# The prologue of an attention + FFN kernel, put in a new order on all engines

## The chip, the cores and the metric

The kernel runs on one core of one Trainium2 chip, as one program with one launch. Its time is the device time in microseconds. Three runs of the kernel before took 350.19, 349.46 and 346.96 us; the median is 349.46.

## What is computed

One pre-norm transformer block over x of shape (2, 1024, 128) in f32, with 16 heads of 8 channels:

```python
x = x + attn(layernorm(x))     # q, k, v = xn @ W.T + b; softmax(q k^T + rel_emb[bucket(i-j)] * SCALE, causal) v, then Wo
x = x + ffn(layernorm(x))      # in the reference only expert 0 has weight 1: relu(t @ w1 + b1) @ w2 + b2
# ffn: z = t + that; (z - mean) * rsqrt(var + 1e-5) * gamma + beta
```

The relative bias of a head depends on i - j alone and is constant beyond a distance of 128, so only a band near the diagonal needs it.

## The kernel before, in words

**Data.** The 2048 rows lie in 16 tiles of 128; a *half* is four tiles (512 columns). Attention is cut into 8 groups of 4 heads, 4 groups for each batch (`G`, `GPB`); groups 0 to 3 are batch 0. Q and K are held as a sum of three bf16 parts (`QS`, `NPART`), written to DRAM (`qk_scratch`) and loaded again in the layout of the matmuls: `QA` and `KA` with two buffers each, by half (`load_q` six transfers, `load_k` four). ScalarE makes the first part from PSUM (`first_parts`), the others come from subtractions: for batch 0 on VectorE (`split`, the third query part on GpSimd), for batch 1 on GpSimd, from copies that ScalarE leaves in `R[1]`.

**A group.** For each group, TensorE computes *units* (42, `job`, L1079): scores of a block of queries against "far" keys and "near" keys (with bias, from `NBH`), of which VectorE takes row maxima into `FM`. After unit 11 and unit 40 the maxima of a half are split into two bf16 terms and transposed (units "m0" and "m1"), VectorE copies them to `mrow`, and SP moves them into two rows of `QA` (`move_m`, L454). Then the 12 *steps* of a group run: `scores` (L1107) with these rows as a subtraction, `biases` (L1123) with the table `TT`, Exp on ScalarE (`exps`, L722), `values` (L1138). Units of the next group are placed between the steps of the current one (`SLOTS`; for group 0 `SLOTS0`). Three PSUM banks hold units, so TensorE can be three units ahead of VectorE. Group 0 is the exception: units 0 to 16 run before its first step, 17 to 20 beside the first scores, 21 to 41 in its steps 0 to 2, and units of group 1 in the rest.

**The prologue.** On TensorE: keep-busy matmuls of zeros (`keep_busy`), the relative bias (`task_f`), for each half transposes (`task_t`), Q and K (`task_qks`), V (`task_v`), then the eight matmuls that lay out the reversed bias table `rev` (`task_flip`), whose results `copy_nbh` moves to `NBH`, even ones on ScalarE, odd ones on VectorE. Then the 17 first units, with batch 1's T, Q/K and V tasks at fixed places between them (`T_AT`, `QK_AT`, `V_AT`: the number is the unit before which a task stands). On ScalarE: square roots, copies and first parts, the K loads of group 0, the loads of `rev` (1 MB, into `PT`) and of `TL` (960 KB, into `OT`), from which four copies make `TT` (`copy_tt`), and at the end one Exp on a single element, ahead of which the Exp table is loaded. On GpSimd: memsets of `KA` and of the ones in `VG`, normalisation of batch 1 (`second_batch_norm`), the bias of V, batch 1's parts, bias rows for x. On SP: loads of x, the stores of batch 0, the Q loads, the row move, both halves of group 1 (Q and K), the stores of batch 1.

**What sets the order.** Every engine runs its instructions in the order written and waits on counting semaphores; each wait holds up all that is behind it. `s_qst[b][c]` counts the stores of a half (b batch, c half), `s_mid` the second parts, `s_q3` the third parts, `s_q1` the first parts, `s_xn` normalised halves, `s_xt` their transposes in SBUF, `s_vc` copies of V, `s_r` copies in `R[1]`, `s_zero` memsets. SP's and ScalarE's DMAs go out through queues of their own (q1 and q10 in the profile), GpSimd's through q0. `task_flip` for banks 0 and 1 waited for both V copies, since V stood in those banks.

## Time and profile before

| | us |
|---|---|
| median of three runs | 349.46 |
| the profiled execution: its time | 348.02 |
| its span, first to last instruction | 346.2 |
| mean granted TensorE clock | 0.938 |
| busy: TensorE 291.8, VectorE 273.9, ScalarE 189.5, GpSimd 86.9 | |

The row of busy tenths in 40 slices (8.66 us each) shows the prologue in the first six or seven digits:

```profile
PE   7855687878999998898999889889899888999980
DVE  5565275688889888888989888898899968748895
ACT  2332198305656756765674685585566568762330
POOL 2114999700220202022022011202200001425351
PEclk9995599756999999999999999999999999999996
DMA  7445502540110112022020113123211102000022
```

A digit is the busy share of a slice in tenths, PEclk the granted clock in tenths of full speed. From about slice 11 on the pattern of the groups repeats; the last slices are the output projection and the FFN. Times below are in us from the start of the span.

### The profile page before, as it was taken

The page shows a single profiled execution, that of the slowest core. Times are in us where ns is not written, and L with a number is a line of the kernel's source. Part 1 is how long each engine was busy: PE and PEld are TensorE (multiplying, and loading weights), DVE is VectorE, ACT ScalarE, POOL GpSimd, SP SyncE. Part 2 cuts the span into 40 slices and gives each one's busy share as a digit, 9 for nine tenths or more (in the row PEclk, how much of TensorE's full clock was granted, in tenths as well). Part 3 has the DMA queues.
Part 4 walks back from the last instruction along what each step waited for, and adds up shares of the span by engine and source line. Part 5 has one row for each costly group of instructions (what it writes and reads, how often), then busy time and mean ns, then how long its engine had stood idle before and what let it go on. Part 6 is the DMA issues. An engine that isn't in the chain of part 4 may idle for free.

```text
span 346.2 us, 8324 instructions
## 1 busy us (share of the span) xinstructions
PE 291.8 (84%) x3233; PEld 130.6 (38%) x3235; DVE 273.9 (79%) x968; ACT 189.5 (55%) x262; POOL 86.9 (25%) x127
## 2 busy tenths in 40 slices
PE   7855687878999998898999889889899888999980
PEld 4421332222334234334334423433433343358650
DVE  5565275688889888888989888898899968748895
ACT  2332198305656756765674685585566568762330
POOL 2114999700220202022022011202200001425351
PEclk9995599756999999999999999999999999999996
DMA  7445502540110112022020113123211102000022
GB/s 213 125 126 151 127 0 65 156 139 1 56 56 3 36 23 56 2 54 56 3 57 29 41 27 78 55 34 75 66 22 24 23 4 42 8 0 17 0 62 61
DMA packets 16263, 18.80 MB, mean 54 GB/s; under 512 B 4480, under 2 KB 11776, under 8 KB 16096
## 3 DMA queue, kind: packets, MB, share of 16 engines
q1 hardware_dynamic: 13488, 12.56, 15.3%
q10 hardware_dynamic: 816, 2.96, 3.0%
q0 software_dynamic: 1920, 2.76, 2.7%
q8 instruction: 25, 0.41, 0.5%
q14 instruction: 14, 0.11, 0.1%
HBM read 11.81 MB, written 4.23 MB: 46 GB/s over the span
## 4 chain that ended last, share of the span: by engine, by line
PE 51%; DVE 19%; ACT 14%; issue 6%; POOL 4%; DMA 3%; SPq 1%; ACTq 1%; DVEq 0%; POOLq 0%
PE ps L1145 16%; PE ps L1101 13%; ACT PT L729 9%; PE ps L1133 7%; PE ps L1116 7%; DVE FM L865 6%; DVE junk L872 3%; ACT TT L687 2%; POOL XN L566 2%; PE ps L1178 2%; PE ps L1034 2%; DVE st L929 2%; DVE U L982 1%; PE ps L1087 1%; DMA table_s<-in_table 1%
## 5 line engine op out<-in xcount | busy, mean ns | idle before, releaser
L729 ACT ACTIVATE PT<-ps 128x1024 f32<-128x1024 f32 (+1 forms) x192 | 144.7, 813 | 93.6 <-PE ps L1133 82.1
L865 DVE TENSOR_REDUCE FM<-ps 128x1 f32<-128x512 f32 (+2 forms) x192 | 109.2, 617 | 14.5 <-PE ps L1101 14.0
L872 DVE CUSTOM_DVE_ANT_0 junk<-ps,NBH 128x256 bf16<-128x256 f32 (+1 forms) x256 | 90.3, 400 | 24.7 <-PE ps L1101 24.5
L1101 PE MATMUL ps<-KA,QA 56*128 56x256 bf16 (+3 forms) x544 | 96.9, 292 | 10.6 <-DVE FM L865 7.4
L1116 PE MATMUL ps<-QA,KA 58*128 58x512 bf16 (+3 forms) x384 | 78.0, 334 | 17.5 <-ACT PT L729 14.6
L1145 PE MATMUL ps<-PT,VG 128*16 128x512 f32 (+3 forms) x768 | 87.3, 500 | 0.1
L1101 PEld LDWEIGHTS ps<-KA,QA 56*128 56x128 bf16 x544 | 33.0, 96 | 97.2 <-DVE FM L865 40.6
L420 POOL DMA_DIRECT2D KA<-qk_scratch x24 | 12.9, 542 | 156.7 <-PE ps L1133 156.4
L1116 PEld LDWEIGHTS ps<-QA,KA 58*128 58x128 bf16 x384 | 25.0, 94 | 37.1 <-ACT PT L729 30.2
L1133 PE MATMUL ps<-TT,flb 128*32 128x176 f16 (+4 forms) x1152 | 38.7, 244 | 0.0
L1133 PEld LDWEIGHTS ps<-TT,flb 128*32 128x32 bf16 x1152 | 21.5, 96 | 17.4 <-issue 15.8
L1145 PEld LDWEIGHTS ps<-PT,VG 128*16 128x16 f32 x768 | 21.6, 97 | 6.3 <-ACT OT L734 2.3
L872 DVE DVE_READ_ACCUMULATOR2_ANT FM<- 128x1 f32 x256 | 20.9, 81 | 0.0
L623 POOL TENSOR_SCALAR tmp<-mv 128x4 f32<-128x4 f32 x8 | 2.3, 290 | 66.7 <-DVE mv L932 66.7
L1178 PE MATMUL ps<-QS,late_s 128*128 128x512 f32 x32 | 15.8, 611 | 0.8 <-ACT QS L756 0.8
L1059 PE MATMUL ps<-idle 128*128 128x512 bf16 x29 | 10.7, 534 | 2.2 <-DVE idle L784 1.2
L424 POOL DMA_DIRECT2D KA<-qk_scratch x24 | 12.4, 520 | 0.0
L1034 PE MATMUL ps<-xnT,early_s 128*128 128x512 f32 x16 | 11.1, 834 | 1.4 <-ACT xnT L658 1.4
L658 ACT COPY xnT<-ps 128x512 f32<-128x512 f32 x4 | 2.3, 586 | 16.6 <-PE ps L1028 16.6
L918 DVE RECIPROCAL xnT<-xnT 128x256 f32<-128x256 f32 (+1 forms) x4 | 10.2, 2538 | 0.0
L938 DVE TENSOR_TENSOR QS<-ps,X 128x512 f32<-128x512 f32 x4 | 2.7, 684 | 8.5 <-PE ps L1169 8.5
L734 ACT COPY OT<-ps 128x512 f32<-128x512 f32 x16 | 9.5, 591 | 0.0
(98 smaller groups left out, 261.1 us busy)
## 6 DMA issues: line engine op xcount, KB each, us to landing
QA<-qk_scratch SPq DMA_DIRECT2D x64, 48.0 KB
KA<-qk_scratch POOLq DMA_DIRECT2D x24, 96.0 KB, 2.7
qk_scratch<-QS SPq DMA_DIRECT2D x8, 192.0 KB
qk_scratch<-QS SPq DMA_DIRECT2D x12, 128.0 KB
...
PT<-fr_scratch ACTq DMA_DIRECT2D x1, 1024.0 KB, 4.7
...
```

What stands on the lines that cost most here:

```text
L420: eng.dma_start(KA[64 * e:64 * e + 48, p, c, :, :].rearrange("r h n -> r (h n)"), bass.AP(qk_d, at + e * TILE, [[LINE, 2 * HD], [0, NPART] ...
L424: eng.dma_start(KA[64 * e + 48:64 * e + KS, p, c, :, :].rearrange("r h n -> r (h n)"), bass.AP(qk_d, at + e * TILE + 2 * HD * LINE, [[LINE ...
L729: nc.scalar.activation(PT[:, s % 3, 2 * q:2 * q + 2, off:off + w], ST[:, q, :, off:off + w], ACT.Exp).then_inc(s_exp, 1)
L865: nc.vector.tensor_reduce(FM[:, ib, heads[0]:heads[-1] + 1:2, piece], bank[:, 0:w * len(heads)].rearrange("p (h n) -> p h n", n=w), AX.X, ...
L872: last = nc.vector.tensor_tensor_reduce(junk[:, n % NSM, i, 0:w], bank[:, i * w:(i + 1) * w], nb[:, h, 256 - w:256], 1.0, NEG, ALU.add, AL ...
L1034: nc.tensor.matmul(ps[:, BANK["QK"[qk], b, c], :], (wq_s, wk_s)[qk][:, :], xnT[:, b, c * IC:(c + 1) * IC], start=True, stop=True).then_inc ...
L1059: nc.tensor.matmul(ps[:, bank, :], idle[:, 0:128], idle[:, :], start=True, stop=True)
L1101: last = nc.tensor.matmul(SM[:, n % NSM, i * w + j - j0:i * w + j - j0 + nj], QA[r0:r0 + KS, p, ib // 4, q, (ib % 4) * 128:(ib % 4 + 1) * ...
L1116: last = nc.tensor.matmul(ST[:, q, e, off:off + w], KA[64 * e:64 * e + KST, p, jb // 4, q, (jb % 4) * 128:(jb % 4 + 1) * 128], QA[64 * e:6 ...
L1133: last = nc.tensor.matmul(ST[r0:r0 + 32, q, h % 2, off:off + n], flb[:, 32 * e:32 * e + 32], TT[:, hg, h, u0:u0 + n], start=False, stop=Tr ...
L1145: last = nc.tensor.matmul(OV[32 * h:32 * h + 2 * HD, off:off + w], VG[:, jb, g, h, :], PT[:, s % 3, h, off:off + w], start=(jb == 0), stop ...
L1178: last = nc.tensor.matmul(bank, w1_s[:, f * 128:(f + 1) * 128], tT[:, c % 2, :], start=True, stop=True)
```

## The change

It is a new order of the prologue; the groups from 1 on and the tail keep theirs.

- TensorE: five keep-busy matmuls fewer at the start, the six ahead of the units gone. Flips 0 to 3 stand ahead of batch 0's V, flips 4 to 7 behind it (V now in banks 2 and 3). Units wait for `s_mid` 4 and the table copies, and no longer for the third parts. Batch 1 goes half by half: T before units 2 and 8, Q/K before 4 and 10, V before 13 and 15.
- VectorE: the two splits of half 0 come before the normalisation of half 1; statistics of batch 1 and table copies 1 and 3 (two instead of four) before the splits of half 1, which now include the third query part.
- ScalarE: first parts of half 0, then the loads of `rev` and `TL` and the load of the Exp table, then half 1; six table copies; T of batch 1; only the K load of half 1. Three of the four `TT` copies move into group 0, between the third and fourth Exp pairs.
- GpSimd: memsets early; it waits for half 0's stores and issues the K load of group 0's half 0, later those of group 1.
- SP: key parts are stored singly as each is ready, group 1's Q loads come before the row move, `late` ahead of batch 1's stores, and the wait for these stores moves to the load that fetches group 4.

```diff
-T_AT = {2: 0, 4: 1}
-QK_AT = {6: ((0, 0), (0, 1)), 8: ((1, 0), (1, 1))}
-V_AT = {10: 0, 12: 1}
+T_AT = {2: 0, 8: 1}
+QK_AT = {4: 0, 10: 1}
+V_AT = {13: 0, 15: 1}
 RECIP_AFTER = (6, 14, 22, 30)
...
         s_mid = sem("s_mid")
+        s_lo = sem("s_lo")
         s_r = sem("s_r")
...
         LOADED_Q, LOADED_K = 16 * 6, 16 * 4
-        LOADED = LOADED_Q + LOADED_K
         STORED = 16 * (HP + NPART)
...
-                sp.wait_ge(s_q3[b][qk], c + 1)
+                if (b, c, qk) == (0, 0, 0):
+                    sp.wait_ge(s_lo, 1)
+                else:
+                    sp.wait_ge(s_q3[b][qk], c + 1 if b or qk else c)
                 at = (2 * c + qk) * SIDE + b * 2 * GPB * TILE
...
                     for a in range(NPART):
-                        sp.dma_start(bass.AP(qk_d, at + a * HD * LINE, [[TILE, 2 * GPB], [IC, HD * HP], [1, IC]]),
-                                     QS[:, b, qk, a, c * IC:(c + 1) * IC]).then_inc(s_qst[b][c], 16)
-            def load_half(g, p, c):
-                load_q(sp, g, p, c)
-                load_k(sp, g, p, c)
+                        store_keys(b, c, a)
+            def store_keys(b, c, a):
+                at = (2 * c + 1) * SIDE + b * 2 * GPB * TILE + a * HD * LINE
+                sp.dma_start(bass.AP(qk_d, at, [[TILE, 2 * GPB], [IC, HD * HP], [1, IC]]),
+                             QS[:, b, 1, a, c * IC:(c + 1) * IC]).then_inc(s_qst[b][c], 16)
...
                              F16[:, part, :, :]).then_inc(s_fst[1], 16)
+            def key_part(c, a):
+                ready, count = ((s_q1, 2 * c + 2), (s_mid, 2 * c + 2), (s_q3[0][1], c + 1))[a]
+                sp.wait_ge(ready, count)
+                store_keys(0, c, a)
+            key_part(0, 0)
+            key_part(0, 1)
             store(0, 0, 0)
-            store(0, 0, 1)
+            key_part(0, 2)
             sp.wait_ge(s_qst[0][0], STORED)
             load_q(sp, 0, 0, 0)
+            key_part(1, 0)
             store(0, 1, 0)
-            store(0, 1, 1)
+            key_part(1, 1)
+            key_part(1, 2)
             sp.wait_ge(s_qst[0][1], STORED)
             load_q(sp, 0, 0, 1)
+            load_q(sp, 1, 1, 0)
+            load_q(sp, 1, 1, 1)
             move_m(0, 0, 0)
-            sp.wait_ge(s_zero, 3)
-            load_half(1, 1, 0)
-            load_half(1, 1, 1)
+            sp.dma_start(late_s[:, :], late).then_inc(s_late, 16)
             for c in range(2):
...
                     store(1, c, qk)
-            sp.dma_start(late_s[:, :], late).then_inc(s_late, 16)
-            for c in range(2):
-                sp.wait_ge(s_qst[1][c], STORED)
...
+                if g + 2 == GPB:
+                    for c in range(2):
+                        sp.wait_ge(s_qst[1][c], STORED)
                 load_q(sp, g + 2, p, 0)
...
             nc.gpsimd.memset(mhalf[:, :], -0.5).then_inc(s_p2, 1)
-            for c in range(2):
-                pool.wait_ge(s_mid, 2 * c + 1)
-                q = QS[:, 0, 0, :, c * IC:(c + 1) * IC]
-                nc.gpsimd.tensor_tensor(q[:, 2, :], R[0][:, 2 * c, :], q[:, 1, :], ALU.subtract).then_inc(s_q3[0][0], 1)
+            ones(1)
+            pool.wait_ge(s_zero, 2)
+            nc.gpsimd.memset(VG[:, :, :, :, HD:2 * HD].rearrange("p t g h d -> p (t g h) d"), 1.0).then_inc(s_zero, 1)
+            pool.wait_ge(s_mid, 1)
+            q = QS[:, 0, 0, :, 0:IC]
+            nc.gpsimd.tensor_tensor(q[:, 2, :], R[0][:, 0, :], q[:, 1, :], ALU.subtract).then_inc(s_lo, 1)
+            pool.wait_ge(s_zero, 3)
+            pool.wait_ge(s_qst[0][0], STORED)
+            load_k(pool, 0, 0, 0, s_ldk)
             pool.wait_ge(s_p2, 1)
...
             second_batch_norm(3)
-            pool.wait_ge(s_xn, 4)
-            ones(1)
-            pool.wait_ge(s_zero, 2)
-            nc.gpsimd.memset(VG[:, :, :, :, HD:2 * HD].rearrange("p t g h d -> p (t g h) d"), 1.0).then_inc(s_zero, 1)
             pool.wait_ge(s_rows, 16)
             add_bv(0)
+            load_k(pool, 1, 1, 0, s_ldk)
+            pool.wait_ge(s_qst[0][1], STORED)
+            load_k(pool, 1, 1, 1, s_ldk)
             for k in range(4):
...
-            for c in range(2):
-                pool.wait_ge(s_qst[1][c], STORED)
             for g in range(G - 1):
...
                     load_k(pool, g + 1, 1 - p, 1, s_ldk)
+                if g + 2 == GPB:
+                    for c in range(2):
+                        pool.wait_ge(s_qst[1][c], STORED)
                 if g + 2 < G:
...
             deviation(1)
+            act.wait_ge(s_early, 16)
+            first_parts(0, 0)
             act.wait_ge(s_fst[0], 16)
             act.dma_start(rev[:, :], bass.AP(fr_d, 0, [[H, 128], [1, 256 * H]])).then_inc(s_rev, 16)
-            act.wait_ge(s_early, 16)
-            first_parts(0, 0)
-            turned(0, 1)
-            first_parts(0, 1)
-            copy_v(0)
-            act.wait_ge(s_zero, 1)
-            act.wait_ge(s_qst[0][0], STORED)
-            load_k(act, 0, 0, 0)
-            for i in range(0, 8, 2):
-                copy_nbh(i)
-            act.wait_ge(s_qst[0][1], STORED)
-            load_k(act, 0, 0, 1)
             act.wait_ge(s_fst[1], 32)
...
                               bass.AP(f16_d, part * BW * H, [[H, 64], [1, NEARU * H]])).then_inc(s_tl, 16)
+            act.wait_ge(s_warm, 1)
+            nc.scalar.activation(warm[:, :], eps[:, :], ACT.Exp).then_inc(s_warm, 1)
+            turned(0, 1)
+            first_parts(0, 1)
+            for i in NBH_ACT:
+                copy_nbh(i)
+            copy_v(0)
             turned(1, 0)
+            act.wait_ge(s_zero, 1)
+            act.wait_ge(s_qst[0][1], STORED)
+            load_k(act, 0, 0, 1)
+            first_parts(1, 0)
             turned(1, 1)
-            first_parts(1, 0)
             act.wait_ge(s_tl, 32)
...
             copy_v(1)
-            for hg in range(1, GPB):
-                copy_tt(hg)
-            act.wait_ge(s_warm, 1)
-            nc.scalar.activation(warm[:, :], eps[:, :], ACT.Exp).then_inc(s_warm, 1)
...
-            def group(g, last=False):
+            def group(g, last=False, first=False):
                 for s in range(NSTEP):
+                    if first and s == FIRST_STEP[1] - 1:
+                        for hg in range(1, GPB):
+                            copy_tt(hg)
                     if s + 1 < NSTEP:
...
                 for p in range(2):
-                    group(2 * r + p)
+                    group(2 * r + p, first=r + p == 0)
             group(G - 2)
...
                                                    ALU.add, ALU.subtract))
-                mid = nc.vector.tensor_copy(q[:, 1, :], R_).then_inc(s_mid, 1)
-                if qk:
+                nc.vector.tensor_copy(q[:, 1, :], R_).then_inc(s_mid, 1)
+                if k:
                     dve.wait_ge(s_mid, k + 1)
-                    nc.vector.tensor_tensor(q[:, 2, :], R_, q[:, 1, :], ALU.subtract).then_inc(s_q3[0][1], 1)
+                    nc.vector.tensor_tensor(q[:, 2, :], R_, q[:, 1, :], ALU.subtract).then_inc(s_q3[0][qk], 1)
...
             stats0(1)
-            norm(1)
             nc.vector.tensor_copy(idb[:, :], idf[:, :]).then_inc(s_cst, 1)
             nc.vector.tensor_copy(flb[:, :], flp[:, :]).then_inc(s_cst, 1)
-            for c in range(2):
-                for qk in range(2):
-                    split(c, qk)
-            for i in range(1, 8, 2):
-                copy_nbh(i)
+            for qk in range(2):
+                split(0, qk)
+            norm(1)
             for k in range(2, 4):
                 stats0(k)
+            for i in NBH_DVE:
+                copy_nbh(i)
+            for qk in range(2):
+                split(1, qk)
...
-            dve.wait_ge(s_nbh, 4)
-            dve.wait_ge(s_nbd, 4)
+            dve.wait_ge(s_nbh, len(NBH_ACT))
+            dve.wait_ge(s_nbd, len(NBH_DVE))
             for g, k in STREAM:
...
                 if FLIP_BANK[i] < 2:
-                    pe.wait_ge(s_vc, 2)
+                    pe.wait_ge(s_xt, FLIP_BANK[i] + 1)
                 if i >= 4:
...
             task_f()
-            keep_busy(5, 7)
+            keep_busy(5, 2)
             pe.wait_ge(s_early, 16)
...
             task_qks(0, 1)
-            task_v(0, 0)
-            task_v(0, 1)
             pe.wait_ge(s_f, 2)
...
             pe.wait_ge(s_rev, 16)
-            for i in range(8):
+            for i in range(4):
                 task_flip(i)
+            pe.wait_ge(s_mid, 2)
+            task_v(0, 0)
+            task_v(0, 1)
+            for i in range(4, 8):
+                task_flip(i)
+            def operands(p, half, n):
+                by_act = (p, half) == (0, 1)
+                pe.wait_ge(s_ldqk[p][half], LOADED_Q * n + (LOADED_K if by_act else 0))
+                if n > 1 or not by_act:
+                    pe.wait_ge(s_ldk[p][half], LOADED_K * (n - by_act))
             def job(g, p, k):
...
                         if later and k in HALF_UNITS:
-                            pe.wait_ge(s_ldqk[1 - p][HALF_UNITS[k]], LOADED + LOADED_Q * (load - 1))
-                            if load > 1:
-                                pe.wait_ge(s_ldk[1 - p][HALF_UNITS[k]], LOADED_K * (load - 1))
+                            operands(1 - p, HALF_UNITS[k], load)
                         job(g + later, 1 - p if later else p, k)
...
-            pe.wait_ge(s_q3[0][1], 2)
-            pe.wait_ge(s_nbh, 4)
-            pe.wait_ge(s_nbd, 4)
-            keep_busy(4, 6)
+            pe.wait_ge(s_mid, 4)
+            pe.wait_ge(s_nbh, len(NBH_ACT))
+            pe.wait_ge(s_nbd, len(NBH_DVE))
             for k in JOBS[:JOBS.index(OWN0)]:
...
                     task_t(1, T_AT[k])
-                for c, qk in QK_AT.get(k, ()):
-                    task_qk(1, c, qk)
+                if k in QK_AT:
+                    pe.wait_ge(s_vc, 2)
+                    task_qks(1, QK_AT[k])
                 if k in V_AT:
...
                 if k in HALF_UNITS:
-                    pe.wait_ge(s_ldqk[0][HALF_UNITS[k]], LOADED)
+                    operands(0, HALF_UNITS[k], 1)
                 job(0, 0, k)
...
     order += [("V", 0, 0), ("V", 0, 1)]
-    order += [("T", 1, 0), ("T", 1, 1), ("Q", 1, 0), ("K", 1, 0), ("Q", 1, 1), ("K", 1, 1), ("V", 1, 0), ("V", 1, 1)]
+    for half in range(2):
+        order += [("T", 1, half), ("Q", 1, half), ("K", 1, half)]
+    order += [("V", 1, 0), ("V", 1, 1)]
     bank = {("F", 0, 0): 6}
     bank.update({("T", 0, 0): 0, ("T", 0, 1): 1, ("Q", 0, 0): 2, ("K", 0, 0): 3, ("Q", 0, 1): 4,
-                 ("K", 0, 1): 5, ("V", 0, 0): 0, ("V", 0, 1): 1,
-                 ("T", 1, 0): 2, ("T", 1, 1): 3, ("Q", 1, 0): 0, ("K", 1, 0): 1, ("Q", 1, 1): 2,
-                 ("K", 1, 1): 3, ("V", 1, 0): 0, ("V", 1, 1): 1})
+                 ("K", 0, 1): 5, ("V", 0, 0): 2, ("V", 0, 1): 3,
+                 ("T", 1, 0): 0, ("T", 1, 1): 1, ("Q", 1, 0): 2, ("K", 1, 0): 3, ("Q", 1, 1): 0,
+                 ("K", 1, 1): 1, ("V", 1, 0): 2, ("V", 1, 1): 3})
     return {t: n for n, t in enumerate(order)}, bank
...
 FLIP_BANK = [6, 7, 0, 1, 6, 7, 0, 1]
+NBH_ACT, NBH_DVE = (0, 2, 4, 5, 6, 7), (1, 3)
...
```

## Rows read from the trace of the kernel before

**Rows 1.** The stages of group 0 and of group 1, busy us of each engine, granted clock, DMA.

```profile
57.70:80.40 22.70, 16.60 (x140) 5.67 (x136) 17.31 (x62) 5.21 (x9) 9.13 (x19) 0.64 0.44 127
80.40:102.40 22.00, 21.02 (x258) 7.93 (x254) 19.41 (x65) 13.46 (x18) 4.37 (x8) 0.90 0.13 37
102.40:131.60 29.20, 26.68 (x378) 11.03 (x368) 26.52 (x98) 18.93 (x27) 3.76 (x9) 1.00 0.12 31
```

**Rows 2.** The chain of waits in order of time: start us, us, what.

```profile
52.39 3.81 ACT TT L687 x2
...
56.22 1.28 ACT L720
...
57.73 1.03 ACT PT L729
...
78.03 1.75 DMA QA<-mrow
```

**Rows 3.** Groups of ScalarE's instructions by line, 43 to 57.75 us: busy, mean ns.

```profile
L687 ACT COPY TT<-OT 128x960 f16<-128x960 f16 x4 | 7.6, 1966 | 0.0
...
L663 ACT ACTIVATE QS<-ps,early_s 128x512 bf16<-128x512 f32 x4 | 2.8, 692 | 1.8 <-PE ps L1034 1.7
```

**Rows 4.** TensorE in order of time: start us, us, instructions, idle before.

```profile
7.05 3.17 PE L1059 MATMUL ps<-idle 128*128 128x512 bf16 x7
...
11.74 3.78 PE L1034 MATMUL ps<-xnT,early_s 128*128 128x512 f32 x4 [0.68 <-ACT xnT L658]
...
17.05 1.98 PE L1034 MATMUL ps<-xnT,early_s 128*128 128x512 f32 x4 [0.68 <-ACT xnT L658]
...
29.08 2.72 PE L1059 MATMUL ps<-idle 128*128 128x512 bf16 x6 [0.88 <-DVE NBH L834]
...
40.92 3.38 PE L1034 MATMUL ps<-xnT,early_s 128*128 128x512 f32 x4
...
55.51 0.39 PE L1116 MATMUL ps<-QA,KA 58*128 58x512 bf16 x2 [0.56 <-issue]
```

**Rows 5.** VectorE in order of time, 14 to 53 us.

```profile
14.64 0.75 DVE L813 SCALAR_TENSOR_TENSOR PT<-ps,early_s,QS 128x512 f32<-128x512 f32 x1 [1.09 <-ACT QS L663]
...
17.07 0.43 DVE L815 CAST QS<-PT 128x512 bf16<-128x512 f32 x1
...
20.84 0.83 DVE L815 CAST QS<-PT 128x512 bf16<-128x512 f32 x1
...
52.50 0.40 DVE L860 COPY mrow<-ps 8x512 bf16<-8x512 bf16 x1
```

**Rows 6.** GpSimd in order of time.

```profile
34.90 0.22 POOL L561 TENSOR_SCALAR tmp<-mv 128x4 f32<-128x4 f32 x1
...
36.35 3.14 POOL L566 TENSOR_SCALAR XN<-X,mv,rs 128x128 f32<-128x128 f32 x4
```

**Rows 7.** DMA issues of SP and of ScalarE in order of time.

```profile
18.43 1.97 SPq L446 DMA_DIRECT2D qk_scratch<-QS  x3
...
23.37 1.64 SPq L408 DMA_DIRECT2D QA<-qk_scratch  x4
...
31.84 1.24 ACTq L420 DMA_DIRECT2D KA<-qk_scratch  x2
```

**Rows 8.** The DMA share in three stretches of the prologue.

```profile
12.00:15.00 3.00, 3.00 (x4) 1.13 (x5) 1.88 (x8) 0.69 (x1) 0.00 (x0) 1.00 0.95 336
18.00:23.00 5.00, 3.80 (x22) 2.36 (x21) 4.18 (x8) 2.55 (x4) 1.16 (x1) 1.00 0.59 159
32.00:41.00 9.00, 3.24 (x21) 1.78 (x17) 2.40 (x16) 0.89 (x2) 8.75 (x11) 0.50 0.67 162
```

**Rows 9.** Transfers, KB each and median us from issue to landing (page, part 6).

```profile
PT<-fr_scratch ACTq DMA_DIRECT2D x1, 1024.0 KB, 4.7
...
KA<-qk_scratch POOLq DMA_DIRECT2D x24, 96.0 KB, 2.7
```

**Rows 10.** ScalarE in order of time, inside group 0.

```profile
80.47 1.94 ACT L729 ACTIVATE PT<-ps 128x1024 f32<-128x1024 f32 x2 [7.54 <-PE ps L1116]
```

## The prediction

> **What bounds the kernel now.** I read the stages first, then the chain of waits, then each engine in order of time over the first 60 us. The steady head group takes 29.2 us at full TensorE clock, with all engines close to busy; the first group takes 22.7 + 22.0 us, and its first stretch has a granted clock of 0.64 [rows 1]. The change touches nothing of the seven later groups or the tail. So all it can win lies ahead of the first exponential of group 0 (57.73) and inside that group. The chain of waits just ahead of that exponential is ScalarE alone: table copies and the load of the Exp table [rows 2]. But it is not alone there: TensorE issued the first scores only at 55.51 [rows 4], behind the row copy of the maxima (52.50 to 52.90 on VectorE [rows 5]), SP's move of it and its landing; from those scores to the exponential lie 2.2 us more (the far and near maxima of units 17 to 20 and the bias matmuls). So two chains end within half a us of each other, and taking the table work off ScalarE is worth nothing unless scores(0,0) comes earlier too. What fed both was batch 1: GpSimd finished its last normalisation at 39.5 [rows 6], and behind it and a transpose came Q/K matmuls at 40.92 [rows 4].
>
> **The change, part by part.**
>
> *First half of batch 0.* Seven keep-busy matmuls took 3.17 us, two remain: 2.2 us less, and the normalised tiles are there by then. The transposes start at 7.9 instead of 10.1; with ScalarE's copy they take 1.7 (to 11.74 before), so Q and K of half 0 run 9.6 to 13.3 (3.78 us for their four passes, against 1.98 for the next four: half rate, although the record of the granted clock gives 1.00 so early [rows 4]). ScalarE's first parts end at 12.4 and 14.1 (0.69 each [rows 3]), VectorE's key split (0.75 + 0.43 and a difference of 0.7 [rows 5]) at 16.0. The stores now go out by parts: key part 0 at 14.1, part 1 at 15.4, queries 16.0 to 17.2, key part 2 from 17.2; an issue is 0.6 us. Before, the last of the five was issued from 19.8 (18.43 plus two issues) and the loads followed at 23.37 [rows 7]: 3.55 us. Unhindered they land at 20.8.
>
> *What it puts beside them.* The 1 MB load of the reversed table moves from 11.1 to 14.1 on ScalarE's queue, the two TL loads from 34 to 14.5. Before, the first had the DMA engines to itself (share 0.95 over 3 us = 2.9 us of work), the five stores took 0.59 x 5 = 3.0, TL and the half-1 loads 0.67 x 9 = 6.0, of which I estimate 4 for TL [rows 8]. All three now start near 16: best 20.8, worst 16 + 2.9 + 4 + 3.0 = 26. I take 24, nearer the worst, because the ScalarE queue holds its work first: later than the 23.37 of before by half a us, so the early stores themselves win nothing. The Trainium skill (DMA: Bandwidth & Descriptors, Queues, rings and completion order) says each engine goes round its queues packet by packet; no row shows it, and by it stores with small packets would land near the worst value.
>
> *Second half of batch 0.* norm(1) now waits on VectorE behind the key split: 16.0 + 1.3 = 17.3 (before 13.3). ScalarE issues three loads and the Exp table load (1.28 + 0.2 [rows 2]) from 14.1 to 17.2, just under that cover. Transpose to 18.4, copy to 18.9, Q/K at half rate to 22.4, first parts to 23.5: 3.7 later than before. Flips 0 to 3 follow on TensorE (the reversed table, 4.7 us after its issue [rows 9], is due at 18.8; 3.9 us of slack), VectorE copies 1 and 3 to 25.1 and then splits both sides, 1.9 each, to 28.9. The six copies and two V copies on ScalarE (0.6 apart, an estimate from the 0.69 of a first part that overlaps its neighbour) end at 30.2, the copies alone at 29.0. Last store issue from 29.0, landed by the same 3.55 at 32.6 (before 31.84 [rows 7]): 0.8 lost.
>
> *GpSimd.* It waits for the store at 24, issues four loads (2.1 us, as ScalarE's four at 31.84 [rows 7]) and then normalises: 4.6 each (34.90 to 39.49 for the last [rows 6]): 30.7 and 35.3 instead of 34.9 and 39.5, 4.2 earlier. The ones and VG memsets move into its idle time before 16: nothing, as VG and KA are needed later. What queues behind its new waits is this normalisation; the batch-1 splits after it have stores that only group 4 needs.
>
> *TensorE's units.* The six keep-busy matmuls (2.72 us at 29.08 [rows 4]) go, and units start when copies 4 to 7 are done and half 0 is loaded (24 + 2.1 + 2.7 [rows 9] = 28.8): 29.1 instead of 31.7. T(1,0) at 30.7 to 31.8, its copy to 32.4, the four K load issues on ScalarE wait for 32.6 and take 2.1 (as in [rows 7]) to 34.7; this is the new wait, and first_parts(1,0) is queued behind it: four of 0.65 to 37.3. turned(1,1) to 37.9. Then Q/K(1,1): 3.4 at half rate [rows 4], to 41.3; units 10 to 12 (0.9), V twice (1.1 each, an estimate from the 1.98 of four Q/K passes), units 13 to 15 between (1.2), m0 0.3: 45.9. Row copy 46.7 behind unit 15's maxima, then 2.6 to the scores as before (52.90 to 55.51): 49.3, plus 2.2: the first exponential at 51.5. With the clock up from 38 on, Q/K take 2.0 and the V matmuls less: 50.0. ScalarE, without three table copies (3 x 1.97 [rows 3]) and the table load, finishes copy_v(1) near 45.5 and no longer counts. I take 50.9: **6.8 earlier**. SP issues the query loads of half 0, half 1 and group 1 (2.3 us for six [rows 7]) up to 39.6, then is free for the row move at 46.7; before, that move stood ahead of group 1's loads. Its wait for batch 1's stores, now left to group 2, hid under the second row move, under way at 78.0 [rows 2]: nothing.
>
> *Three table copies in group 0.* 5.9 us of ScalarE ahead of exps(0,4). There ScalarE sat idle 7.54 us before 80.47 [rows 10], behind maxima, m1 and the mrow move (a landing of 1.75 us [rows 2]). 1.6 us of cover is left: cost 0, and up to 5.9 if that idle time vanished. TensorE needs table 1 only at the end of the group.
>
> *Small ones.* A VectorE cast beside a GpSimd subtraction took 0.83 instead of 0.43 [rows 5], twice in the new order at most: 0.8 us, inside VectorE's slack (not in the sum). By the Trainium skill (SBUF — State Buffer, Who interferes with whom) a two-port cast and GpSimd lock each other out; that row agrees.
>
> Sum: 6.8 less. The profiled execution took 348.02 us, 1.44 under the median of 349.46 of the three runs. 348.02 - 6.8 = 341.2; against the median 342.7. I give **342**.
>
> **The rivals.**
> 1. *Loads crowd the stores out* (0.14). If half 0 lands at 26 or later and TL still runs beside the K loads, GpSimd ends near 38 and unit 0 starts past 31; each us goes through to T(1,0) and half of it to the exponential. With a store landing at 27 and half 1 at 36 the exponential is at 54 to 55: 3 to 4 gained, 345 to 346.5. For it: 10 us of transfer work from 16 on [rows 8]. Against: TensorE and ScalarE have 1 to 2 us of slack there.
> 2. *More than the sum* (0.14). TensorE is denser from 29 on, and if its clock stays up, then also group 0's first stretch (0.64 now [rows 1]) shortens: exponential at 49 and up to 4 us inside the group: 10 to 12, so 337 to 338. Against: before, the Q/K matmuls at 40.92 still ran at half rate [rows 4].
> 3. *The table copies become the wait* (0.07). If group 0 gets to exps(0,4) faster by 3 us or more, the 5.9 us stick out and give back 1.5 to 4: 343.5 to 346.
> 4. *Slower* (0.07): the reversed table's load. Flips stand behind it on TensorE, and behind them V, both split copies, the second half's stores, ScalarE's K load and all of batch 1. It decides from 22.4 on, one for one: landed at 29.2 (15 us after issue instead of 4.7) the gain is gone, at 33.5 the time is 353. For it: it has to share with stores and TL. Against: even all the work in line ends at 26, which would cost 3.6.
> 5. *No effect* (0.03): the change doesn't do what it says, because scores(0,0) stay tied to 55.5 by GpSimd's store wait (it equals the old start of its normalisation if half 0 landed at 28); 348 to 349.
>
> Forecast as worked out, 339.5 to 344.5: 0.55. **Range** 337 to 347: late landings (rival 1) and rival 3 reach up to 346.5, the clock (rival 2) down to 337. A measurement of this kernel can tell about 1% from no change. Under 346: the forecast, rival 2, 3 and most of rival 1: 0.82. Within 1%: 0.11. Over 353: 0.07.
>
> **What would show it.** The first exponential (L729's successor) at 50 to 52; half-0 loads beginning at 21 to 26; GpSimd's last normalisation by 36 to 38; no idle time of ScalarE left but little before exps(0,4), with 5.9 us of table copies in it; group 1 starting about 7 earlier and every later group at 29.2 as before. It is wrong if scores(0,0) still come after 54 (then the wait ahead of m0 tells which rival), or if group 0 takes more than 46 us.

## The result, and the profile after

The changed kernel takes 344.68 us in the median of 20 runs, against 349.79 of the kernel before in as many runs beside it: a ratio of 0.9875, 95% interval 0.9851 to 0.9900, so 1.0 to 1.5% less. The profiled execution took 342.63 us with a span of 340.8 (before 348.02 and 346.2).

The page of the kernel after, parts 2 and 4: the granted clock in 40 slices (8.5 us each) in tenths, and the shares of the engines in the chain of work that ended last.

```profile
PEclk9967698969999999999999999999999999999997
...
PE 52%; DVE 22%; ACT 11%; issue 6%; DMA 4%; POOL 3%; SPq 1%; DVEq 0%; POOLq 0%
```

In the slices up to the tenth the clock reads 6, 7 and 6 in the third to fifth and 8 and 6 in the seventh and ninth; before it read 5 and 5 in the fourth and fifth and 7, 5 and 6 from the eighth on.

The stages that answer to [rows 1]: from the first exponential to the one of step 4, from there to the first of group 1, and group 1. Columns: stretch, length, busy us (and count) of PE, PEld, DVE, ACT, POOL, granted clock, DMA share, GB/s.

```profile
53.30:74.10 20.80, 14.36 (x142) 5.13 (x138) 17.08 (x62) 10.65 (x12) 12.13 (x22) 0.83 0.24 72
74.10:96.00 21.90, 20.52 (x253) 7.83 (x252) 19.40 (x65) 13.43 (x17) 4.15 (x8) 0.93 0.13 39
96.00:125.20 29.20, 26.68 (x378) 11.03 (x368) 26.51 (x98) 18.92 (x27) 3.69 (x8) 1.00 0.10 29
```

The gain is ahead of group 1 and nowhere else, and it has two parts. The first exponential comes at 53.30 instead of 57.73: 4.4 earlier. And the stretch from it to the exponential of step 4 is 20.8 instead of 22.7, with a granted clock of 0.83 instead of 0.64: 2.0 more. The second stretch and group 1 have their old lengths (21.9, 29.2). 6.4 in all; the last VectorE instruction is 6.4 earlier too (336.3 + 0.5 against 342.7 + 0.5), and so is the landing of the last output (339.1 against 345.5). But the span is only 5.4 shorter, because it doesn't end with that landing. It ends 0.2 us behind GpSimd's last long instruction, a DRAIN, which took 5.09 us before and 6.07 now. In all 14 traces of this case it is 5.09 where GpSimd issued 48 DMAs (the kernel before, e4) and 6.07 where it issued 60 (all others). The change gives GpSimd twelve more (three K loads of four issues each); no run changed their number alone, so the link is likely and not shown.

Up to 0.5 of the 4.4 may not be the change's: the table's load landed sooner in this execution (TensorE's first use of it at 3.83 instead of 4.38). In e3 below, where that use is at 4.25, the first exponential comes 0.4 later than here.

The 2.0 are those of two single executions. The traced one of the kernel after is the fastest of its 20 (342.63), and the traced one of the kernel before lies 1.8 under its median; how much of the 5.1 us between the medians is clock is not shown.

ScalarE of the kernel after, in order of time: start, us, instructions, idle before them and what ended it.

```profile
14.43 1.28 ACT L719 ACT_TABLE_LOAD   x1 [0.90 <-issue]
...
34.37 0.58 ACT L676 COPY xnT<-ps 128x512 f32<-128x512 f32 x1 [5.79 <-PE ps L1046]
34.79 1.29 ACTq L420 DMA_DIRECT2D KA<-qk_scratch  x2
...
53.30 1.94 ACT L743 ACTIVATE PT<-ps 128x1024 f32<-128x1024 f32 x2 [5.98 <-PE ps L1162]
...
67.19 5.55 ACT L705 COPY TT<-OT 128x960 f16<-128x960 f16 x3
74.08 1.94 ACT L743 ACTIVATE PT<-ps 128x1024 f32<-128x1024 f32 x2 [1.34 <-PE ps L1145]
```

Where ScalarE had no idle time ahead of the first exponential [rows 2, 3], it now waits 5.98 us for TensorE. The three table copies lie in what was 7.54 of idle time [rows 10]; 1.34 is left of it.

TensorE of the kernel after, answering to [rows 4]:

```profile
9.33 3.48 PE L1052 MATMUL ps<-xnT,early_s 128*128 128x512 f32 x4 [0.68 <-ACT xnT L676]
...
30.69 0.40 PE L1130 MATMUL ps<-KA,QA 56*128 56x128 bf16 x4 [4.54 <-DMA KA<-qk_scratch]
33.22 1.11 PE L1046 MATMUL ps<-early_s,XN 128*128 128x128 f32 x4 [2.13 <-POOL XN L579]
...
35.10 3.75 PE L1052 MATMUL ps<-xnT,early_s 128*128 128x512 f32 x4 [0.22 <-ACT xnT L676]
...
41.44 1.96 PE L1052 MATMUL ps<-xnT,early_s 128*128 128x512 f32 x4 [0.34 <-ACT xnT L676]
...
47.75 2.77 PE L1077 MATMUL ps<-idle 128*128 128x512 bf16 x12
51.08 0.39 PE L1145 MATMUL ps<-QA,KA 58*128 58x512 bf16 x2 [0.57 <-issue]
```

TensorE waits for the load of half 0 (4.54) and for GpSimd's normalisation (2.13), and both come of the same landing: SP's queue and GpSimd, answering to [rows 7] and [rows 6].

```profile
16.99 0.61 SPq L454 DMA_DIRECT2D qk_scratch<-QS  x1
25.37 1.56 SPq L408 DMA_DIRECT2D QA<-qk_scratch  x4
...
27.65 0.61 SPq L454 DMA_DIRECT2D qk_scratch<-QS  x1
...
29.55 1.80 SPq L454 DMA_DIRECT2D qk_scratch<-QS  x2
34.73 1.52 SPq L408 DMA_DIRECT2D QA<-qk_scratch  x4
```

```profile
25.98 1.49 POOL L420 DMA_DIRECT2D KA<-qk_scratch  x2 [11.31 <-DMA qk_scratch<-QS]
...
30.03 3.14 POOL L579 TENSOR_SCALAR XN<-X,mv,rs 128x128 f32<-128x128 f32 x4
...
34.60 3.12 POOL L579 TENSOR_SCALAR XN<-X,mv,rs 128x128 f32<-128x128 f32 x4
```

The last store of half 0 is issued at 16.99, and only at 25.37 does SP load it back: 8.4 us, the longest piece of the chain of waits.

### The profile page after: what moved, and what is told of

It is laid out like the page before. It is cut to its first block, busy times and chain, and to the rows that moved or that the text cites. A ratio compares the mean times of both kernels' runs of the same rounds, so it can differ in the third digit from the quotient of the medians.

```text
span 340.8 us, 8308 instructions
## 1 busy us (share of the span) xinstructions
PE 286.3 (84%) x3224; PEld 129.0 (38%) x3224; DVE 272.6 (80%) x967; ACT 190.3 (56%) x264; POOL 92.0 (27%) x138
## 4 chain that ended last, share of the span: by engine, by line
PE 52%; DVE 22%; ACT 11%; issue 6%; DMA 4%; POOL 3%; SPq 1%; DVEq 0%; POOLq 0%
PE ps L1174 15%; PE ps L1130 12%; ACT PT L743 9%; DVE FM L883 8%; PE ps L1145 8%; PE ps L1162 7%; DVE junk L890 4%; PE ps L1052 3%; DMA qk_scratch<-QS 2%; PE ps L1207 2%; DVE st L947 2%; DVE U L1000 1%; PE ps L1116 1%; PE ps L1077 1%; DVE xnT L913 1%
## 5 line engine op out<-in xcount | busy, mean ns | idle before, releaser
L1174 PE MATMUL ps<-PT,VG 128*16 128x512 f32 (+3 forms) x768 | 86.1, 493 | 0.1
L1130 PEld LDWEIGHTS ps<-KA,QA 56*128 56x128 bf16 x544 | 33.3, 95 | 99.8 <-DVE FM L883 42.1
L420 POOL DMA_DIRECT2D KA<-qk_scratch x30 | 16.4, 550 | 163.3 <-PE ps L1162 151.9
L1174 PEld LDWEIGHTS ps<-PT,VG 128*16 128x16 f32 x768 | 21.5, 97 | 6.1 <-ACT OT L748 2.3
L424 POOL DMA_DIRECT2D KA<-qk_scratch x30 | 15.5, 528 | 0.0
L1052 PE MATMUL ps<-xnT,early_s 128*128 128x512 f32 x16 | 13.0, 958 | 1.9 <-ACT xnT L676 1.9
L681 ACT ACTIVATE QS<-ps,early_s 128x512 bf16<-128x512 f32 x8 | 5.5, 692 | 8.2 <-PE ps L1052 8.2
L1046 PE MATMUL ps<-early_s,XN 128*128 128x128 f32 x16 | 4.0, 396 | 6.3 <-DVE XN L820 4.2
```

The source lines that it names most:

```text
L420: eng.dma_start(KA[64 * e:64 * e + 48, p, c, :, :].rearrange("r h n -> r (h n)"), bass.AP(qk_d, at + e * TILE, [[LINE, 2 * HD], [0, NPART] ...
L424: eng.dma_start(KA[64 * e + 48:64 * e + KS, p, c, :, :].rearrange("r h n -> r (h n)"), bass.AP(qk_d, at + e * TILE + 2 * HD * LINE, [[LINE ...
L1052: nc.tensor.matmul(ps[:, BANK["QK"[qk], b, c], :], (wq_s, wk_s)[qk][:, :], xnT[:, b, c * IC:(c + 1) * IC], start=True, stop=True).then_inc ...
L1130: last = nc.tensor.matmul(SM[:, n % NSM, i * w + j - j0:i * w + j - j0 + nj], QA[r0:r0 + KS, p, ib // 4, q, (ib % 4) * 128:(ib % 4 + 1) * ...
L1174: last = nc.tensor.matmul(OV[32 * h:32 * h + 2 * HD, off:off + w], VG[:, jb, g, h, :], PT[:, s % 3, h, off:off + w], start=(jb == 0), stop ...
```

## The experiments

Every kernel is the changed one with one edit, except where it says so. All were timed beside the kernel before; a ratio is to it. The last three columns are from one profiled execution of each, in us from its start; "step 4" is the exponential that stands behind the table copies. There are 5 to 12 runs of each kernel, 20 of the kernel after; beside the experiments the kernel before had medians of 349.62 to 349.71. The profiled execution is the first of its runs and not the middle one: it took 345.43 in e5, 341.86 in e8, and the longest time of its six in e9 (347.22) and e10 (342.36). So a column can be off by the clock of that one run, and the medians decide.

```
kernel              median   ratio [95%]              first exp  step 4  group 1
before              349.79                            57.73      80.47   102.39
after               344.68   0.9875 [0.9851, 0.9900]  53.30      74.08   96.00
e12_old_places      350.92   1.0046 [1.0011, 1.0081]  59.81      82.50   104.43
e4_tables_only      349.15   1.0010 [0.9979, 1.0042]  59.61      80.43   103.42
e3_copies_back      344.11   0.9864 [0.9810, 0.9919]  53.69      76.03   98.01
e1_tl_late          344.57   0.9880 [0.9825, 0.9935]  52.51      73.96   95.89
e2_both_loads       342.40   0.9818 [0.9766, 0.9870]  52.22      73.88   95.81
e5_norm_first       343.49   0.9822 [0.9772, 0.9872]  54.21      76.87   98.80
e7_norm1_first      344.37   0.9863 [0.9828, 0.9897]  53.56      75.41   97.34
e8_best             340.33   0.9755 [0.9709, 0.9800]  50.71      73.26   95.19
e10_tl_last         341.70   0.9786 [0.9735, 0.9837]  50.33      72.89   95.80
e11_busy            340.65   0.9777 [0.9724, 0.9830]  50.24      71.69   93.61
e9_no_idle_mm       345.86   0.9907 [0.9875, 0.9940]  54.57      78.43   100.54
e13_busy_only       344.70   0.9891 [0.9855, 0.9927]  54.16      74.91   96.84
```

**What carries the gain: batch 1's places.** The tasks of batch 1 go back behind the units where they stood, both halves' transposes first.

```diff
-T_AT = {2: 0, 8: 1}
-QK_AT = {4: 0, 10: 1}
-V_AT = {13: 0, 15: 1}
+T_AT = {2: 0, 4: 1}
+QK_AT = {6: 0, 8: 1}
+V_AT = {10: 0, 12: 1}
...
-    for half in range(2):
-        order += [("T", 1, half), ("Q", 1, half), ("K", 1, half)]
+    order += [("T", 1, 0), ("T", 1, 1), ("Q", 1, 0), ("K", 1, 0), ("Q", 1, 1), ("K", 1, 1)]
```

> The changed kernel with batch 1's tasks back at the units of the kernel before (T before units 2 and 4, all Q/K before 6 and 8, V before 10 and 12). Theory P (the placing half by half is what gains: Q/K of half 0 run at 35.1 while GpSimd still normalises half 1): TensorE waits at unit 4 for the normalisation that ends at 37.7, Q/K of half 0 start at 39.5, the first exponential comes 2 to 3.5 us later, at 55.5 to 57, half to three quarters of the gain gone. Rival R (the gain comes from the earlier normalisation and the dropped idle matmuls, whatever the places): under 1 us lost.

350.92 in the median: the whole gain is gone, and a little more. The first exponential is 6.5 us later, about twice what was expected. TensorE of this kernel, in order of time:

```profile
33.69 1.11 PE L1046 MATMUL ps<-early_s,XN 128*128 128x128 f32 x4 [2.69 <-POOL XN L579]
...
38.26 1.11 PE L1046 MATMUL ps<-early_s,XN 128*128 128x128 f32 x4 [2.90 <-POOL XN L579]
...
39.63 3.32 PE L1052 MATMUL ps<-xnT,early_s 128*128 128x512 f32 x4
...
44.87 1.96 PE L1052 MATMUL ps<-xnT,early_s 128*128 128x512 f32 x4 [1.59 <-ACT xnT L676]
...
52.65 0.50 PE L1130 MATMUL ps<-KA,QA 56*128 56x384 bf16 x1 [2.19 <-DVE FM L883]
```

The first transpose comes at 33.69, as late as in the kernel after (33.22); but Q/K of half 0 have to wait for the second half's normalisation (idle 2.90) and start at 39.63 instead of 35.10. That is 4.5 of the 6.5. The rest is lost further on: 1.59 ahead of the second half's Q/K, because ScalarE keeps its new order, with first_parts(1,0) ahead of the second half's copy, and 2.19 ahead of the last unit. That unit is done at 53.15 instead of about 47.1. So e12 is not quite the old placing: it has the old places with ScalarE's order for the new ones. The placement half by half is necessary for the gain, and the order ahead of unit 0 (half 0 early, stores by parts, the loads moved) did not show one without it. That the placement would be enough in the old order wasn't tried.

**Is the table work worth nothing?** Two kernels. The first is the kernel before with only the copies moved into group 0 and the load of the Exp table moved up; the second is the kernel after with the three copies back ahead of the first exponential.

```diff
 # e4, on the kernel before
             copy_v(0)
+            act.wait_ge(s_warm, 1)
+            nc.scalar.activation(warm[:, :], eps[:, :], ACT.Exp).then_inc(s_warm, 1)
...
             copy_v(1)
-            for hg in range(1, GPB):
-                copy_tt(hg)
-            act.wait_ge(s_warm, 1)
-            nc.scalar.activation(warm[:, :], eps[:, :], ACT.Exp).then_inc(s_warm, 1)
...
+                    if first and s == FIRST_STEP[1] - 1:
+                        for hg in range(1, GPB):
+                            copy_tt(hg)
...
 # e3, on the kernel after
             copy_v(1)
+            for hg in range(1, GPB):
+                copy_tt(hg)
...
-                    if first and s == FIRST_STEP[1] - 1:
-                        for hg in range(1, GPB):
-                            copy_tt(hg)
```

> The kernel before with nothing but ScalarE's table work moved: three table copies into group 0, Exp table load right behind the V copies of batch 0. Theory A: the scores at 55.5 and their maxima still hold the first exponential at 57.5, so 0 to 0.3 us gained, ratio 1.000 to the kernel before. Rival T: 5 to 7 us gained, ratio 0.983.

> The changed kernel with the three table copies back ahead of the first exponential (5.7 us on ScalarE from 47.3 on); the Exp table load stays early. Theory A (scores, not ScalarE, set the first exponential; ScalarE sat idle 5.98 us before it): first exponential at 53.3 to 53.5, time unchanged within 0.1 %. Rival T (the table copies out of the way are what the change gains): first exponential 5.7 us later, 1.6 % slower than the changed kernel.

Neither moves the time: 1.0010 with an interval on both sides of 1, and 344.11 against 344.68. ScalarE of e3:

```profile
47.59 5.60 ACT L705 COPY TT<-OT 128x960 f16<-128x960 f16 x3
53.69 1.94 ACT L745 ACTIVATE PT<-ps 128x1024 f32<-128x1024 f32 x2 [0.50 <-PE ps L1161]
...
76.03 1.94 ACT L745 ACTIVATE PT<-ps 128x1024 f32<-128x1024 f32 x2 [7.42 <-PE ps L1144]
```

With the copies back there are still 0.50 us in which ScalarE waits for TensorE: the scores set the start, and the copies fit under them. They are a second chain that ends half a us sooner, as [rows 2, 4] had shown it of the kernel before. In e4 ScalarE, rid of all table work, waits 10.59 us for the scores. They come at 57.38 there, 1.9 later than before, and the exponential with them, at 59.61 and not at the expected 57.5: twelve idle matmuls ahead of them ran at half rate, 5.00 us instead of 2.54 for eleven. Step 4 comes at 80.43, as before, since the stretch behind is shorter by the same amount (20.8 at a granted clock of 0.77). TensorE of e4:

```profile
52.45 5.00 PE L1060 MATMUL ps<-idle 128*128 128x512 bf16 x12
57.38 0.39 PE L1117 MATMUL ps<-QA,KA 58*128 58x512 bf16 x2
```

**Do the table loads crowd the stores out?** e1 issues the two TL loads only behind ScalarE's first two flip copies; e2 issues the reversed table's load ahead of first_parts(0, 0) as well.

In the cuts from here on, a comment line that names a load stands for the lines that issue it.

```diff
+            # e2 only: the rev load here, ahead of the wait for s_early
             act.wait_ge(s_early, 16)
             first_parts(0, 0)
-            # e2 only: rev load
-            # both TL loads
...
             first_parts(0, 1)
+            for i in NBH_ACT[:2]:
+                copy_nbh(i)
+            act.wait_ge(s_fst[1], 32)
+            # both TL loads
-            for i in NBH_ACT:
+            for i in NBH_ACT[2:]:
                 copy_nbh(i)
```

> The changed kernel with one edit: the two TL loads (960 KB) are issued behind the first two table copies of ScalarE, at about 24, instead of at 13.2 beside the stores of half 0. Theory A (the 2 MB on ScalarE's queue holds the stores back): the stores of half 0, 8.4 us from last issue to landing in the changed kernel, land 2 to 4 us sooner, at 21.5 to 23.5 instead of 25.35; half 0's units start at about 28 instead of 30.7 and the first exponential comes at 51 to 52 instead of 53.3, 0.4 to 0.6 % faster than the changed kernel. Rival B (the landing is slow for another reason, such as the stores by parts): landing stays at 25, no gain.

> As e1, and the load of the reversed table (1 MB) goes back ahead of the first parts of half 0 (issued at about 9.9 instead of 12.85). Theory A: nothing large is left beside the stores, they take the 3.5 us of the kernel before and land at 20.5 to 21; units start when the eight table copies are done (27.6), the second half's stores land at 31.5 instead of 34.7, the first exponential at 50, some 3 us (0.9 %) faster than the changed kernel. Rival B: no change. Rival C (batch 1's normalisation on GpSimd sets the first scores whatever the stores do): units start early but the first exponential moves by less than 1 us.

Yes: the last store of half 0 now lands 3.9 us after its issue (e1) and 3.3 (e2) instead of 8.4. SP of e2:

```profile
17.23 0.61 SPq L454 DMA_DIRECT2D qk_scratch<-QS  x1
20.56 1.56 SPq L408 DMA_DIRECT2D QA<-qk_scratch  x4
...
33.28 1.52 SPq L408 DMA_DIRECT2D QA<-qk_scratch  x4
```

But of the 4.8 us by which half 0 lands sooner in e2, 1.1 arrive at the first exponential (52.22, where 50 was expected). TensorE of e2 shows where the rest goes:

```profile
27.61 0.29 PE L1132 MATMUL ps<-KA,QA 56*128 56x128 bf16 x4 [1.54 <-ACT NBH L696]
...
38.79 3.38 PE L1054 MATMUL ps<-xnT,early_s 128*128 128x512 f32 x4 [1.93 <-ACT xnT L676]
```

Unit 0 starts 3.1 sooner, now behind the flip copies; but Q/K of batch 1's second half start only 2.6 sooner and at half rate (3.38 instead of 1.96), because ScalarE's four K load issues still stand behind half 1's stores, which land at 33.3, 1.4 sooner. In e1 the late loads take the place of the crowding: unit 0 waits to 30.24 for GpSimd's K load, issued from 22.47 on, with TL in flight beside it. So e1 gains nothing in the median; e2 gains 2.3 us, with intervals that overlap (0.9766 to 0.9870 against 0.9851 to 0.9900).

**GpSimd's wait, and VectorE's order.** e5 puts half of batch 1's normalisation ahead of GpSimd's wait for the store; e7 puts norm(1) ahead of the key split on VectorE.

```diff
 # e5
+            pool.wait_ge(s_p2, 1)
+            second_batch_norm(2)
             pool.wait_ge(s_qst[0][0], STORED)
             load_k(pool, 0, 0, 0, s_ldk)
 # e7
+            norm(1)
             for qk in range(2):
                 split(0, qk)
-            norm(1)
```

> The changed kernel with batch 1's first normalisation on GpSimd ahead of the wait for half 0's stores (GpSimd sat idle there for 11.3 us; its statistics are ready at 19.3). Theory D (the new wait in front of batch 1's work delays it): the first transpose of batch 1 comes right behind units 0 and 1, at about 31 instead of 33.2, the second at 38 instead of 40; but ScalarE's K load still waits for the stores of half 1 at 34.7 with batch 1's first parts behind it, so the first exponential gains 0.5 to 1.5 us (0.2 to 0.4 %). Rival C (GpSimd's normalisation is the whole chain): gains 2 us or more.

> The changed kernel with the normalisation of half 1 back ahead of the splits on VectorE, where 2.4 us were idle (9.8 to 12.2). Theory: T of half 1 at 13 instead of 17, its Q and K done at about 20 instead of 22.6 (ScalarE has the Exp table load in between), table copies and splits up to 2 us earlier if the reversed table, issued at 12.85 with 3 MB in flight, has landed by 20; half 1's stores at 33.5 instead of 34.7 and the first exponential 1 us earlier. If the reversed table lands only at 22, nothing is gained before the flips, and that would show that its load had no slack left.

Neither stands out alone: 343.49 and 344.37, and neither first exponential is earlier (54.21, 53.56). e5 has its second normalisation done at 33.3 instead of 37.7, yet Q/K(1,1) come at 40.02, behind ScalarE's wait for half 1 (34.5), and take 3.57 instead of 1.96. e7 has the second half's Q/K at 17.13 instead of 18.77, but half 0 still lands at 25.80, half 1 at 34.19 (expected: 33.5), since half 1's stores queue behind SP's loads of half 0. Each takes away a wait ahead of another one with the same end.

**All of them together.** e8 joins e2, e5 and e7, with turned(0, 1) also ahead of the load of the Exp table.

```diff
 # ScalarE
+            turned(0, 1)
             act.wait_ge(s_warm, 1)
             nc.scalar.activation(warm[:, :], eps[:, :], ACT.Exp).then_inc(s_warm, 1)
-            turned(0, 1)
```

> All together: both loads moved as in e2, normalisation of half 1 ahead of the splits, its copy on ScalarE ahead of the Exp table load, batch 1's first normalisation ahead of the wait for the stores. Units start at 27, stores of half 1 land at 30, the first exponential at 49.7 (52.2 in e2): some 2.5 us less than e2, ratio to the kernel before about 0.975. Against it: GpSimd issues the K load of half 0 later (22.2), and the TensorE clock may fall in the stretch before the scores, which would give back 2 us in the idle matmuls ahead of them.

340.33, ratio 0.9755: the interval [0.9709, 0.9800] lies clear of that of the change. It has the lowest median of all versions, 4.3 us under the changed kernel and 9.5 under the one before, though its interval overlaps those of e2, e5, e10 and e11. GpSimd and TensorE of e8:

```profile
19.13 3.31 POOL L579 TENSOR_SCALAR XN<-X,mv,rs 128x128 f32<-128x128 f32 x4
22.39 1.47 POOL L420 DMA_DIRECT2D KA<-qk_scratch  x2
```

```profile
30.01 0.40 PE L1132 MATMUL ps<-KA,QA 56*128 56x128 bf16 x4 [7.60 <-DMA KA<-qk_scratch]
```

SP's loads of half 0 go out at 21.11 and those of half 1 at 31.56, GpSimd has its second normalisation done at 29.5, and the first exponential is at 50.71: 2.6 sooner than in the kernel after, 1.0 later than expected. What is left is the 7.60 us in which TensorE waits for GpSimd's K load, beside TL again: 27 was expected for unit 0.

**The next wait.** e10 is e8 with TL behind turned(1, 1) and copy_tt(0) behind copy_v(1); e11 is e10 with twelve keep-busy matmuls ahead of unit 0; e13 is the kernel after with these twelve alone.

```diff
 # e10
             turned(1, 1)
+            # both TL loads
-            act.wait_ge(s_tl, 32)
-            copy_tt(0)
             first_parts(1, 1)
             copy_v(1)
+            act.wait_ge(s_tl, 32)
+            copy_tt(0)
...
 # e11, e13, on TensorE
             pe.wait_ge(s_nbd, len(NBH_DVE))
+            keep_busy(4, 12)
```

> As e8, but the two TL loads are issued behind the copy of batch 1's second transpose (about 36) and the first table copy stands behind the V copies of batch 1. In e8 TensorE waited 7.6 us for the K load of half 0, issued at 22.4 beside TL and landed at 30. Theory A (TL delays whatever it flies beside): the K load lands at 27 to 27.5, units start there, half 1's stores land at 30, and the first exponential comes at 48 to 49 instead of 50.7: 1.5 to 2.5 us (0.6 %) faster than e8. Rival: the landing stays near 30 because GpSimd's own DMAs are slow, no gain; or TL now lands late (after 45) and its copy holds the scores up.

> As e10, with 12 idle matmuls on TensorE in the wait ahead of unit 0 (2.6 us at full clock, hidden under that wait). Theory K (the clock falls in that wait and Q/K of batch 1's first half then take 3.75 instead of 1.96 us): Q/K at full rate, first exponential 1 to 1.8 us earlier than in e10, and group 0's first steps faster. Rival: they end after the operands have landed or run at half rate (5 us), no gain or 1 us lost.

> The changed kernel with 12 idle matmuls in the 4.5 us that TensorE waits ahead of unit 0 (the kernel before had six there; the change dropped them). Theory K: they run at full clock from 27.6 to 30.3, units start at 30.7 as before, Q/K at 35.1 may run at full rate if the clock holds over the next wait (31 to 33.2): 0 to 1.8 us earlier first exponential. Rival: the clock has fallen before Q/K again, no change.

In e10 the K load lands 2.9 sooner (unit 0 at 27.12), but Q/K(1,1) take 3.75 instead of 1.96 and the exponential is at 50.33, where 48 to 49 was expected; the median is 341.70. Nothing beyond the spread. e11 and e13 were to keep the clock up. TensorE of e11:

```profile
22.65 4.09 PE L1077 MATMUL ps<-idle 128*128 128x512 bf16 x12 [2.53 <-DVE QS L832]
...
28.57 1.95 PE L1052 MATMUL ps<-xnT,early_s 128*128 128x512 f32 x4 [0.36 <-ACT xnT L676]
...
35.90 3.75 PE L1052 MATMUL ps<-xnT,early_s 128*128 128x512 f32 x4 [3.24 <-ACT xnT L676]
```

They do it for Q/K(1,0), 1.95; then TensorE waits 3.24 us for ScalarE and the next four passes run at half rate. The exponential is at 50.24, as in e10. Its profile is the shortest of all (span 338.4), its median (340.65) is as good as e8's. e13 has Q/K(1,0) still at 3.26, its first exponential 0.9 later than in the kernel after, and 344.70: no change.

**The keep-busy matmuls ahead of the scores.** Twelve of them stand between unit 15 and the scores, where TensorE has nothing to do.

```diff
-            keep_busy(1, 12)
```

> The changed kernel without the 12 idle matmuls ahead of the first scores (2.77 us; they took 5.00 at half rate in e4). Theory: in a run with full clock there they are hidden by the move of the maxima's rows (scores 0 to 0.5 us earlier without them); in a run with half clock they cost 1.5 us. But without them the clock may fall before group 0, whose first steps then run at half rate: median between 1 us faster and 2 us slower than the changed kernel; if slower, the idle matmuls pay for themselves.

Without them 345.86, 1.2 more in the median, with intervals that overlap (0.9875 to 0.9940). In the trace TensorE's work from unit 0 to 48.2 takes as long as in the kernel after (1.96 for the last four Q/K passes); then it idles, and the scores already run slower (0.61 instead of 0.39):

```profile
51.52 0.61 PE L1145 MATMUL ps<-QA,KA 58*128 58x512 bf16 x2 [3.30 <-issue]
```

The window of e9 from its first exponential to that of step 4:

```profile
54.60:78.40 23.80, 19.04 (x141) 6.44 (x137) 16.93 (x62) 10.61 (x11) 11.22 (x21) 0.50 0.17 52
```

The same instructions take 23.8 us at a granted clock of 0.50, against 20.8 at 0.83 in the kernel after. PE's busy time grows from 14.4 to 19.0. But these are the slowest run of e9's six beside the fastest of the kernel after's twenty, so the 3.0 us are an upper end; 1.2 is what the medians give.

## Why the prediction was right, step by step

The predicted 342 is 2.7 below the measured 344.68, and 344.68 is inside the range of 337 to 347. Against the profile the sum said 341.2 and 342.63 was measured. The mechanism held, but the chain up to the first exponential was 2.4 us too short, the group behind it 2.0 too long, and the end of the program 1.0 too short. That the total is off by so little is in part luck: the 2.0 came by the clock of one run, which the sum didn't count on.

```
step                               predicted   measured
T(0,0) starts                      7.9         7.56
Q/K of half 0                      9.6-13.3    9.33-12.81
VectorE's key split ends           16.0        15.68
stores of half 0 landed            24          25.35
Q/K of half 1 done                 22.4        22.55
splits of half 1 done              28.9        28.09
GpSimd's K load landed             28.8        30.6
stores of half 1 landed            32.6        34.7
GpSimd's normalisations end        30.7, 35.3  33.2, 37.7
ScalarE's K load issues end        34.7        37.15
Q/K(1,1) start                     38          41.44
maxima's m0 done                   45.9        47.67
scores(0,0)                        49.3        51.08
first exponential                  50.9        53.30
idle time left ahead of step 4     1.6         1.34
first exponential to group 1       44.7        42.70
```

**Right.** The first half's timing, to 0.4 us. That the early stores win nothing by themselves: they go out sooner and land 2 us later than before [rows 7] (e12 agrees, as far as it goes). That the table work was worth nothing, in either place (e3, e4), with 1.34 us of cover left against 1.6. That seven groups keep their 29.2 [rows 1], and the work behind them its length. That ScalarE's K load becomes a new wait, with first_parts(1,0) behind it.

**Mis-sized: the landing of half 0.** 24 was taken between 20.8 and 26, and it was 25.35. In the trace after, the page's median for the reversed table's load is 5.6 us against the 4.7 of [rows 9], and for the TL loads 8.3 against 6.4 before:

```profile
OT<-f_scratch ACTq DMA_DIRECT2D x2, 480.0 KB, 8.3
```

The DMA engines are 0.89 to 1.00 busy in each 2 us from 14 to 22 and 0.68 from 22 to 24. That is the first rival's mechanism at work, short of its threshold (26); e1 and e2 show it by taking it away. The worst value, all three in line from 16 on, was nearly reached, and 24 was too low a pick, by the very argument that the prediction gave (ScalarE's queue holds its work first). The Trainium skill (DMA: Bandwidth & Descriptors, Queues, rings and completion order) has each DMA engine go round its queues by packets, so that neither goes first; the landing near the worst value agrees with that, but no run here separates its order from another one.

**Mis-sized: what hangs on it.** From the landing to GpSimd's first issue went 0.6 and the four issues took 2.5, not 2.1, so the normalisation starts 2.4 late and ends 2.4 late. The K load itself took 4.7 from its first issue to unit 0, near the 2.1 plus 2.7 of the prediction. And half 1's stores were predicted at splits plus 3.55; SP issued key part 0 only at 27.65, behind its six loads of half 0 (25.37 to 27.6), and the last two parts at 29.55 to 31.35. The prediction counted what each queue is moved past, but set the last issue by VectorE (29.0) and not by SP. It is 2.1 late, and ScalarE's four issues with it. From there to Q/K(1,1) another 1.0 went by, in two waits of ScalarE for TensorE (0.43 and 0.56) that the sum didn't have.

**Left out: the end of the program.** The prediction says that the change touches nothing of the tail. The last VectorE instruction agrees with that, 6.4 earlier like group 1. But GpSimd's last instruction takes 6.07 instead of 5.09 us and ends the span: 1.0 us that the sum put at nothing.

**The clock, twice.** Q/K(1,1) start 3.4 late, but m0 is only 1.8 late: they took 1.96 instead of 3.4. And the first stretch of group 0 took 20.8 instead of 22.7. This is half of the second rival (group 0 shorter), given a chance of 0.14 as a case of its own, and not in the sum. It goes with the clock and not with the copies. In the 14 traces this stretch takes 20.8 us at a granted clock of 0.77 to 0.83 (after, e13, e4), 21.5 to 21.9 at 0.67 to 0.71, 22.3 to 22.7 at 0.62 to 0.65, and 23.9 at 0.50 (e9). Where the copies stand doesn't sort them: without the copies in it the stretch is 22.74 before and 22.34 in e3, with them it is 20.8 in e4 and 22.7 in e5 and e12. The two traces with the most and the least differ in 12 matmuls that compute nothing.

Whole runs lean the same way, less clearly. Of 51 runs of the kernel before that were timed beside the experiments, nine had a mean granted clock of 0.942 to 0.948 and took 345.5 to 348.1; the other 42 had 0.931 to 0.938, and 40 of them took 348.8 to 351.8, but two took 347.5 and 347.8. The change does not make its shorter stretch certain: its 20 runs go from 342.63, the profiled one, to 346.9.

So: 6.8 predicted; 4.4 of it came by the step named and 2.0 by the clock, less 1.0 at the end of the program.

**The other rivals.** The table copies didn't become a wait (1.34 left), the flips didn't wait for the reversed table (22.34 for the first, no idle time ahead of it), and scores(0,0) left 55.5. VectorE's cast beside GpSimd's subtraction took 0.60 against 0.43 for the one before it:

```profile
13.01 0.43 DVE L832 CAST QS<-PT 128x512 bf16<-128x512 f32 x1
...
14.35 0.60 DVE L832 CAST QS<-PT 128x512 bf16<-128x512 f32 x1
```

That happened once, for 0.2 us; in [rows 5] it was 0.83.

**What stays open.** How e8's 4.3 us divide between its four edits: three were run alone and gave 0.3 to 2.3 in medians whose intervals overlap with the kernel after's, the fourth (turned(0,1) ahead of the table load) wasn't, and they were seen to cover for each other. Why the clock takes one course in some runs and another in others; no run controlled it, so its share of the medians' 5.1 us is open. And whether it is the twelve more DMA issues that lengthen GpSimd's last instruction.
